# Expert products of a GNN plus mixture layer: first expert matrix in two quarter slots, refilled from memory in every block

## The reference, cut to what matters

```python
x = x + gnn(layernorm(x), ...)                     # graph layer: all rows are needed before its last norm
grouped = layernorm(x).reshape(B, S // 16, 16, D)  # groups of 16 tokens, D = 512
cont_logits = einsum('bgtd,des->bgtes', grouped, controller) + tie
cont_perm = cont_logits == max over the 16 tokens  # each (expert, set) takes one token of the group
intermediate = einsum('bgtd,desf->bgtesf', grouped, f1)
inner = relu(einsum('bgtesf,bgtes->bgesf', intermediate, cont_perm))   # f = 32
inter2 = einsum('bgesf,esfd->bgesd', inner, f2)
result = einsum('bgesd,bgtes->bgtd', inter2, cont_perm)
x = x + result
```

## Time and profile before

| | us |
|---|---|
| median of 3 runs | 2023.17 (2020.66 to 2024.76) |
| the profiled execution, its own time | 2016.82 |
| its span, first to last instruction | 2015.1 |
| graph layer, up to the first step of mixture | about 1165 |
| inner 0 of block 0 starts | 1224.5 |
| inner 0 of block 9 (the last) starts | 1957.5 |

### The profile page before, as it was taken

The page is one execution under the profiler, slowest core; times in us unless marked ns, Lnnn a source line. Parts: engine busy times, 40 slices in busy tenths (PEclk is TensorE's granted clock), DMA queues, the critical chain, the costliest instruction groups (busy, mean ns, idle before and its releaser), DMA issues. The chain is left out here.

```text
span 2015.1 us, 41123 instructions
## 1 busy us (share of the span) xinstructions
PE 1842.8 (91%) x15824; PEld 1350.1 (67%) x15824; DVE 1187.9 (59%) x2345; ACT 988.8 (49%) x1715; POOL 362.8 (18%) x428
## 2 busy tenths in 40 slices
PE   5486599999999979999999968999999999999999
PEld 3354478888888858888888865656666566666554
DVE  6486466666666443333333265766767767667665
ACT  2355123333333265565565344656656657556553
POOL 4486220000000000000000042222222222222210
PEclk9678799999999989999999999999999999999999
DMA  9987755566666353343343174534444435344322
GB/s 367 293 146 102 173 163 163 163 184 183 182 176 170 112 193 123 129 170 128 122 169 136 56 270 152 153 117 127 142 127 133 142 112 157 116 128 137 106 76 69
DMA packets 162346, 305.66 MB, mean 152 GB/s; under 512 B 15418, under 2 KB 87098, under 8 KB 159003
## 3 DMA queue, kind: packets, MB, share of 16 engines
q1 hardware_dynamic: 153240, 282.66, 44.5%
q0 software_dynamic: 8960, 20.98, 5.5%
HBM read 168.72 MB, written 134.87 MB: 151 GB/s over the span
## 5 line engine op out<-in xcount | busy, mean ns | idle before, releaser
L1434 PE MATMUL bank<-f2s,inner_bd 128*32 128x512 f32 x2528 | 297.2, 597 | 4.6 <-issue 3.7
L1318 ACT ACTIVATE inter_hi<-bank 128x512 fp32r<-128x512 f32 x316 | 189.1, 598 | 194.8 <-PE bank L1434 192.4
L571 ACT ACTIVATE h1o<-bank,b_by_channel 128x500 f32<-128x500 f32 x160 | 108.7, 679 | 327.1 <-PE bank L386 327.1
L384 PE MATMUL bank<-ahi,w_hi 128*128 128x500 f32 x640 | 250.8, 392 | 14.4 <-DVE alo L725 14.4
L1240 DVE TENSOR_TENSOR inter_lo<-bank,inter_hi 128x512 fp32r<-128x512 f32 x316 | 216.3, 690 | 78.7 <-ACT inter_hi L1318 77.7
L384 PE MATMUL bank<-hhi,w_hi 128*128 128x500 f32 x640 | 251.5, 393 | 2.7 <-DVE hlo L532 2.7
L386 PE MATMUL bank<-hhi,w_lo 128*128 128x500 f32 x640 | 249.9, 390 | 0.0
L385 PE MATMUL bank<-hlo,w_hi 128*128 128x500 f32 x640 | 249.5, 390 | 0.0
L385 PE MATMUL bank<-alo,w_hi 128*128 128x500 f32 x640 | 249.2, 389 | 0.0
L386 PE MATMUL bank<-ahi,w_lo 128*128 128x500 f32 x640 | 248.9, 389 | 0.0
L538 DVE BATCH_NORM_STATS2 stats<-h1o 128x500 f32 (+1 forms) x160 | 103.6, 676 | 162.9 <-ACT h1o L571 162.9
(11 more groups left out here) (133 smaller groups left out, 3188.6 us busy)
## 6 DMA issues: line engine op xcount, KB each, us to landing
h1T<-h1o SPq DMA_DIRECT2D x19, 2000.0 KB, 8.1
h1in<-h1T SPq DMA_DIRECT2D x19, 2000.0 KB, 9.6
aggregate<-zeros SPq DMA_DIRECT2D x20, 1024.0 KB, 9.1
x<-in_x SPq DMA_DIRECT2D x79, 256.0 KB, 2.6
x<-x SPq DMA_DIRECT2D x79, 256.0 KB, 3.4
x_back<-x SPq DMA_DIRECT2D x79, 256.0 KB, 2.9
out<-x_back SPq DMA_DIRECT2D x79, 256.0 KB, 2.1
h2in<-h2T SPq DMA_DIRECT2D x39, 512.0 KB, 4.2
```

The costliest lines, as they stand in the source:

```text
L384: nc.tensor.matmul(out, w_hi[:, k, cols], a_hi[:, k, :], start=(k == 0), stop=False)
L571: nc.scalar.activation(h1o[b][:, m, :], mb[m % 4][:, 0:CW], ACT.Identity, bias=b1c[:, m:m + 1]).then_inc(evr, 1)
L1318: nc.scalar.activation(ihi[n % QB][:, :], bI[n % QB][:, :], ACT.Copy).then_inc(ihr, 1)
L1434: last = nc.tensor.matmul(bI[b][32 * i:32 * i + 32, :], ibd[:, e, j, :, :].rearrange("p s g -> p (s g)"), f2s[:, e, :], start=True, stop=True)
```

## The change

Three things are changed together.

1. f1s holds two quarters (two slots of 1 MB, half as much memory as before). Quarter q lies in slot q % 2. After a quarter was read, SP loads the quarter after next into its slot, in two halves of 512 KB: the first half waits until PE has gone through the first two row groups (semaphore f1h), the second until the quarter is done (inp). In each block all four quarters are loaded anew. PE waits for each half before it reads it. In block 0 the four initial pieces are the halves of quarters 0 and 1: 512 KB each in place of 1 MB.
2. Inside a quarter the order of the products is two halves of 32, so that the first half needs only the first row groups, and inner 0 starts on half of the last tile's yT.
3. Steps are moved: inner 0 ahead of the last tile's final; turn_x of the next front tile from behind sums to a place between unit 1 and inner 3; norm ahead of unit 0. The banks that the four quarters write are other ones (bQ).

```diff
-        f1s = sb("f1s", [P, KH, ES * FF])
+        QC = NE // QB * NS * FF
+        f1s = sb("f1s", [P, 2, KH, QC])
...
+        bQ = [bD[0], bI[2], bD[0], bD[1]]
...
                 if behind and m == 0:
                     yield "inner", 1
+                    if next_:
+                        yield "norm", m + 2
                     yield "unit", u
                     yield "low", u
-                    if next_:
-                        yield "norm", m + 2
                     if new:
                         yield "turn_g", m + 3
                     yield "inner", 2
@@
+                    if next_:
+                        yield "turn_x", m + 2
                     yield "inner", 3
...
                     if ahead:
                         yield "sums", m
-                    if next_:
-                        yield "turn_x", m + 2
...
+                last = m == max(tiles(front), tiles(back)) - 1
+                if last and front is not None:
+                    yield "inner", 0
                 if behind:
                     yield "final", m
                     yield "result", m
-            if front is not None:
-                yield "inner", 0
...
+                def load_f1(k, q, half):
+                    c = slice(2 * half, 2 * half + 2)
+                    rows = f1[2 * half * P:(2 * half + 2) * P, QE * q:QE * q + QE]
+                    sp.dma_start(f1s[:, q % 2, c, :], rows.rearrange("(c p) e s f -> p c (e s f)", p=P))\
+                        .then_inc(wf1[q % 2][half], 16)
+
+                def refill_f1(k, q):
+                    done = k * QB + q + 1
+                    k, q = (k, q + 2) if q + 2 < QB else (k + 1, q - 2)
+                    if k < NB:
+                        sp.wait_ge(f1h, done)
+                        load_f1(k, q, 0)
+                        sp.wait_ge(inp, done)
+                        load_f1(k, q, 1)
+
                 def load_weights(i):
                     if i < KH:
-                        sp.dma_start(f1s[:, i, :], f1[i * P:(i + 1) * P].rearrange("p e s f -> p (e s f)")).then_inc(wf1, 16)
+                        load_f1(0, i // 2, i % 2)
...
+                        if what == "inner":
+                            refill_f1(block_of(n, k, kb), n)
...
+                    for half in range(2):
+                        if q == 0:
+                            done = (k * TB + tiles(k)) * KH
+                            pe.wait_ge(yr, done if half or static(k, 1) else done - KH // 2)
+                        pe.wait_ge(wf1[q % 2][half], 16 * (f1_uses(k, q) + 1))
+                        for e in range(QE * q, QE * q + QE):
+                            for c in (2 * half, 2 * half + 1):
```

More of the change, by code:

```diff
@@ L840, in mixture @@
         bY, bF = [bD, bI[0:2]], bD[1]
+        bQ = [bD[0], bI[2], bD[0], bD[1]]
         bL, bP = bB[:, 0:P], bB[:, 0:P]
-        wctl, wf1, wf2 = sem("controller_loaded"), sem("f1_loaded"), sem("f2_loaded")
+        wctl, wf2 = sem("controller_loaded"), sem("f2_loaded")
+        wf1 = [[sem(f"f1_loaded{i}_{h}") for h in range(2)] for i in range(2)]
+        f1h = sem("f1_first_half_read")
         nrm = [sem(n) for n in ("h2_agg", "h2_var_eps", "h2_rstd", "scale2_ready", "mean_scaled2", "shift2_ready")]
@@ L861, in mixture @@
         CONSTP = 4
+        QE = NE // QB
         PIECES = 4
@@ L884, in mixture @@
         UNITS = TB * QB
-        QE = NE // QB
         def exists(k, j):
@@ L897, in pair_size, with f1_uses @@
             return 2 if exists(k, 2 * p + 1) else 1
+        def f1_uses(k, q):
+            return k * (QB // 2) + q // 2
         def schedule(front, back):
@@ L1009, in schedule @@
                     yield "result", m
-            if front is not None:
-                yield "inner", 0
         def relu(op, q, s, *more):
             return op(ibd[32 * s:32 * s + 32, QE * q:QE * q + QE, :, s, :],
-                      bD[q % 2][32 * s:32 * s + 32, 0:QE * TB * GB].rearrange("p (e j g) -> p e j g", e=QE, g=GB), *more)
+                      bQ[q][32 * s:32 * s + 32, 0:QE * TB * GB].rearrange("p (e j g) -> p e j g", e=QE, g=GB), *more)
         def unit_of(kb, u):
@@ L1450, in inner @@
                 def inner(k, q):
[L1452 to L1469, removed]
@@ L1470, in inner @@
-                    last.then_inc(inp, 1)
+                    if q == 1 and not static(k, 1):
+                        pe.wait_ge(ilr, unit_of(k, 0))
+                    if q == 2:
+                        pe.wait_ge(inv, (k * QB + 1) * 2)
+                        pe.wait_ge(ina, (k * QB + 1) * 2)
+                    if q == 3 and not static(k, 1):
+                        pe.wait_ge(otr, k * TB)
+                    for half in range(2):
[5 more added lines that the diff above has]
+                            for c in (2 * half, 2 * half + 1):
+                                for s in range(NS):
+                                    es = e * NS + s
+                                    last = nc.tensor.matmul(
+                                        bQ[q][32 * s:32 * s + 32, (e % QE) * 64:(e % QE) * 64 + 64],
+                                        f1s[:, q % 2, c, (es * FF) % QC:(es * FF) % QC + FF], yT[:, c, es, :],
+                                        start=(c == 0 and e % QE == 0), stop=(c == KH - 1 and e % QE == QE - 1))
+                        last.then_inc(inp if half else f1h, 1)
```

## The result

The changed kernel takes 2045.46 us (median of 4 runs, 2041.18 to 2048.33), the kernel before 2022.26 in the runs beside it (4 runs, 2020.66 to 2024.76): a ratio of 1.0118, with a 95% interval of 1.0103 to 1.0133. It is 23 us slower. The forecast was 2032 with a range of 2010 to 2044: the sign is right, the size is too small, and the time lies 1.5 us above the range.

The account below looks back on a forecast made before the run. PE was taken as bound by waits, mostly for 16 KB instruction packets fetched behind earlier data. Nine borders +13, the way to block 0's inner 0 -5, block 0's rest +0.5: +8.5 us, a 2032 us median, range 2010 to 2044.

Parts of the forecast that it names:

- The rival that the fetch is served in turn: DMA engines alternate between data and instruction queues, so 1 MB of backlog delays no fetch: 2010 us; chance 25%.
- Late refills, the other rival: 2 KB rows come at half rate, quarters land late: 4 to 5 us per border, +40, 2060; chance 6%.
- A: Instruction packet from inner 0 into inner 1: final's work fills its period, so wait 0 (0 to 0.4) us.
- B: Instruction packet into inner 2: fetch behind x_back's rest and quarter 3's first half, wait 1.0 (0.3 to 2.0) us.
- C: Instruction packet into inner 3: fetch behind x, h2in, x and part of next quarter 0, wait 2.2 (0.9 to 3.1) us.
- issue in nine borders: PE's waits for instruction packets in the borders after block 0's: 3.2 us per border in place of 2.4.
- final's wait for yT: PE's wait ahead of final for ACT's copy of yT: to rise from 4.3 to about 10 us.
- block 0's border: Border without final, 4.8 us of instruction waits before: a count of 4.9, no change, +-2.
- The front: Way to inner 0 of block 0: 2 MB fewer to load shortens it, -5 (-1 to -6) us.
- Both fit, the second barely: Landing of quarters 2 and 3 within some 8 and 7 us from first issue to need: cost 0.
- Inner 0 ahead of final: Final's 1.9 us of work moves behind inner 0, removing the wait into inner 1, some 0.9 us per border.
- turn_x: Moved ahead of inner 3: adds 0.66 us per border, gives back at most as much in C.

Follow-up runs that it names:

- late_refill: Changed kernel, but SP issues the refills of the next block's quarters 0 and 1 later, at the rows steps of tiles 2 and 4; 2041.5 us, ratio 1.0106.
- late_all: late_refill, with SP also holding back x's load, h2in's load and x's store until inner 3 is done; 2024.86 us, ratio 1.0019.
- moves_only: Changed kernel with f1s whole on chip and no refills; moved steps, halves and new banks stay; 2014.37 us, ratio 0.9965.
- inner0_only: moves_only with turn_x and norm back at their old places, so only inner 0 is moved; 2010.97 us, ratio 0.9947.
- moves_late_loads: moves_only with x's load, h2in's load and x's store issued only after inner 3, as in late_all; 2002.34 us, ratio 0.9910.

## Why the prediction was right in sign and too small in size

Its frame held. PE's packets of 256 instructions, one fetched ahead, and a fetch that waits for data issued before it: the earlier trace rows showed it once in the kernel before, and the pair late_refill and late_all shows it by taking the data away. The rival that the fetch is served in turn falls with it. The round robin between queue rows that the Trainium skill states (DMA: Bandwidth & Descriptors, "Queues, rings and completion order") would let a packet through within a fraction of the backlog; the trace does not agree: here it came after 2.6 us at 99.5% of data. Late refills, the other rival, were 2.7 us in one place, not 4 to 5 in each border.

By the steps of the sum, each against the trace, in us:

| step | predicted | measured |
|---|---|---|
| A, wait in inner 1, blocks 1 to 9 | 0 | 0 |
| B, wait in inner 2, per border | 1.0 | 0.6 |
| C, wait in inner 3, per border | 2.2 | 2.9 |
| issue in nine borders, against 21.7 before | 28.8 | 31.6 |
| final's wait for yT, more than before | 5.9 | 4.6 |
| block 0's border, against 4.8 before | 5.3 | 5.6 |
| inner 0 of block 0 earlier by | 5 | 1.5 (0.8 in mixture) |
| refills that land late | 0 | 2.7 |
| the same matmuls, longer | not in the sum | 12.0 |

- **The term that was missing is the largest.** "The change neither adds nor removes a matmul, so the waits decide" is the sentence that failed. In eight of the nine borders of the changed kernel TensorE is at half its clock for some us behind the stop of C (2.15 to 3.72 us; in the last border 1.29 behind the 2.74 of the refill), and this costs as much as all the added waits for issue (12.0 against 10.7). The rows that I showed had the sign of it: behind the stop of 3.45 us in block 0, 41 matmuls take 1.38 us, 34 ns each, and the 33 before it 21 each. I read the length of that stop and not the work behind it. Outside block 0 the longest stop of before was 2.53 us, and the clock stayed up behind it.
- **C was sized by one transfer too few.** I took 1.5 to 3.0 us of data ahead of the fetch and the middle of it; in late_refill 2.8 us were ahead with no refill of the next block at all. B was a little too large. Together they are 31.6 - 28.8 = 2.8 us.
- **The front was 3.5 us too large.** The chain of the earlier trace rows runs over x's loads and stores, and I took it for the time that would be saved. With 2 MB fewer DVE hardly waits for x any more (1166 us to inner 0, kernel before; L1178 adds x to turn_g's product):

```profile
DVE x L1178 <- DMA x<-in_x: 10.2, 5, 2.5
```

In the changed kernel it is one wait of 2.1 us, and at the same place DVE waits for PE's turn_g instead, 5.6 us in place of 2.9. The waits of PE on the way to inner 0 stay as they were (changed kernel, 1166 to 1223; L1372 is turn_g, L1402 turn_p):

```profile
PE bank L1372 <- ACT h2in L1319: 8.7, 6, 1.6
PE bank L1402 <- DVE perm_new L1239: 4.2, 3, 1.6
```

The same two were 8.8 and 3.6 us before. So the earlier loads gave DVE only slack; PE, ACT and DVE, each waiting for the other's last step, set the time. From the first turn_g (1167.39 before, 1166.73 in the changed kernel) to inner 0 it is 57.1 and 56.3 us: mixture gave 0.8 of the 1.5 us, the graph layer ahead of it the rest. With 1 MB pieces inner 0 of block 0 started between 1224.1 and 1227.5 in the kernels above, with 512 KB pieces between 1223.0 and 1225.6.
- **The late refill** of 2.7 us is in the last border, in inner 3. "Both fit, the second barely" came true where I had not looked. Ahead of the last block's expert products SP waits until all earlier stores of out have landed (2.4 us in the trace), and only then issues x_back and the refill: at 1988.74, 4.0 us after the start of inner 1, against 1.2 us in the border of blocks 0 and 1 (1313.36 and 1312.16). Without turn_g and turn_x the way from inner 1 to inner 3 is also 1 us shorter (6.8 against 7.8).
- **Inner 0 ahead of final** and **turn_x** did what the steps said: the first removes A's wait (moves_only, inner0_only), the second, moved together with norm, gives back only what it costs.

The missing 12.0, C and B (2.8), the front (3.5), the refill (2.7) and block 0 (0.3), less 1.3 for yT, are 20.0 us, which is what lies between 8.5 and the 28.5 that the trace adds up to.

What stays open: when the clock falls behind a stop and when not. Of the nine stops of C in the changed kernel, that of 3.10 us in the border of blocks 1 and 2 was followed by the full clock, those of 2.73 and 3.39 us by about half of it (0.57 from 1324 to 1328, 0.54 from 1659 to 1666), and even one of 2.15 us (1913.52) by the lower level from 1915 to 1918. In late_refill the one of 2.97 us shown above was followed by the full clock: 72 matmuls took 1.21 us (17 ns each). In inner0_only one of 3.03 us in block 0 was, too (41 matmuls in 0.78 us). And 11 us more of issue in late_all than in moves_late_loads are put down to the refills as they are left there, quarters 2 and 3 in the border and the others later, by that pair; no kernel here takes those apart, and none shows where the 5.7 us of PE's busy time come from.

## What to carry to other kernels

Where PE runs through many small matmuls, its instructions are a transfer like any other: count them in packets of 256, and keep other transfers from being issued in the few microseconds before and during such a run. Here, issuing three loads and stores after the dense run instead of within it, and putting eight long products between the first two quarters (with the halves and banks), makes the kernel 1% faster than before (2000.85 us), while the changed kernel, with 4 MB of refills per block around the same run, is 1.2% slower. And when a change lengthens a stop of PE, price the clock behind the stop as well as the stop.

## What the runs showed of the hardware

- An instruction packet waits until data issued ahead of it in another queue have gone: 2.6 us at 99.5% (changed kernel), 2.8 us at 98.5% (late_refill). With 1 MB less ahead, the packet starts 1.65 in place of 3.9 us after PE's entry, and the stop is 0.47 in place of 2.97 us (late_all, late_refill, one border).
- After a stop of 2.73 us TensorE ran from 1324 to 1328 at a granted clock of 0.57: 27 ns in place of 18 for a product of 64 columns, 231 ns (3.00 us for 13) in place of some 140 (2.25 us for 16, at the full clock in late_refill) for one of 512 columns. Stops of 3.10 us (changed kernel) and 2.97 us (late_refill) were followed by the full clock.
- In the changed kernel the lower level came behind seven of the eight C stops of 2.15 to 3.72 us, the shortest among them.
- Refills of 512 KB in rows of 2 KB take 5.4 us to land in the median, h2in's 512 KB took 4.2.
